# Attention projections laid out evenly, the next input converted a period earlier, and half of the value strips moved to the middle of a pair

## What is computed

```python
q = proj(wq, bq); k = proj(wk, bk); v = proj(wv, bv)          # x: 4 x 1024 x 512, 16 heads of 32
scores = jnp.einsum('bhqd,bhkd->bhqk', q, k) / scale
probs = jax.nn.softmax(scores, axis=-1)
ctx = jnp.einsum('bhqk,bhkd->bhqd', probs, v)
x = _layernorm(x + ctx.transpose(0, 2, 1, 3).reshape(B, S, HIDDEN) @ wo.T + bo)
x = _layernorm(x + ffn(x))      # top-2 of 8 experts, plus a gated shared expert
```

## Time and profile before

| what | value |
|---|---|
| median of three runs | 2179.62 us |
| the profiled execution | 2177.76 us |
| its span | 2176.0 us |
| PE busy | 2070.3 us, 95% |
| DVE, POOL, ACT busy | 1283.6, 880.2, 856.1 us |
| DMA | 205.91 MB |

### The profile page before, as it was taken

The page is one execution under the profiler, slowest core; times in us unless marked ns, Lnnn a source line. Parts: engine busy times, 40 slices in busy tenths (PEclk is TensorE's granted clock), DMA queues, the critical chain, the costliest instruction groups (busy, mean ns, idle before and its releaser), DMA issues. The chain is left out here.

```text
span 2176.0 us, 29929 instructions
## 1 busy us (share of the span) xinstructions
PE 2070.3 (95%) x9636; PEld 1208.4 (56%) x9637; DVE 1283.6 (59%) x2247; ACT 856.1 (39%) x1506; POOL 880.2 (40%) x852
## 2 busy tenths in 40 slices
PE   7999999999999999999999988789999999999997
PEld 5655555555555555455555433468744444446886
DVE  5777776577776477777477854456222222224875
ACT  2265554365554265554266663321111111112332
POOL 2254754454854454754354554400111111113651
PEclk9999999999999999999999999899999999999999
DMA  5321434212433312433303302661222222224752
GB/s 164 69 54 41 103 74 100 100 42 52 103 74 91 110 27 68 103 74 77 123 19 66 74 11 91 220 271 49 87 88 91 91 87 87 92 87 141 230 181 73
DMA packets 94816, 205.91 MB, mean 95 GB/s; under 512 B 24608, under 2 KB 25120, under 8 KB 92256
## 3 DMA queue, kind: packets, MB, share of 16 engines
q1 hardware_dynamic: 83888, 168.90, 26.6%
q0 software_dynamic: 10800, 35.40, 6.0%
HBM read 113.53 MB, written 39.85 MB: 70 GB/s over the span
## 5 line engine op out<-in xcount | busy, mean ns | idle before, releaser
L826 DVE TENSOR_REDUCE max_half<-ps_side 128x1 f32<-128x512 f32 x1024 | 668.7, 683 | 235.0 <-PE ps_side L584 231.8
L744 ACT ACTIVATE probs_outer<-ps_s 128x512 f32<-128x512 f32 x646 | 375.8, 599 | 245.5 <-PE ps_s L606 212.1
L606 PE MATMUL ps_s<-kq_stack 97*128 97x512 f32 x962 | 412.4, 431 | 15.2 <-ACT probs_mid L744 8.6
L584 PE MATMUL ps_side<-kq_stack 96*128 96x512 f32 x1024 | 404.0, 403 | 3.8 <-DVE max_half L826 2.4
L606 PEld LDWEIGHTS ps_s<-kq_stack 97*128 97x128 f32 x962 | 182.2, 189 | 206.7 <-issue 115.1
L1490 PE MATMUL ps_gu<-gu_sb,xT_e 128*128 x568 | 257.7, 596 | 0.5 <-issue 0.3
L1388 POOL DMA_INDIRECT x_g<-x,who_all x71 | 67.3, 948 | 454.6 <-PE ps_t L1480 358.4
L744 ACT ACTIVATE probs_mid<-ps_s 128x512 f32<-128x512 f32 x316 | 182.1, 599 | 128.9 <-PE ps_s L606 111.5
L522 POOL TENSOR_TENSOR acc<-probs_outer,probs_mid 128x512 f32<-128x512 f32 x129 | 163.5, 1296 | 154.7 <-ACT probs_mid L744 154.3
L584 PEld LDWEIGHTS ps_side<-kq_stack 96*128 96x128 f32 x1024 | 195.0, 190 | 49.7 <-DVE max_half L826 14.6
L522 POOL TENSOR_TENSOR acc<-probs_outer 128x512 f32<-128x512 f32 x129 | 162.8, 1289 | 138.8 <-ACT probs_outer L744 137.7
(11 more groups left out here) (210 smaller groups left out, 3037.0 us busy)
## 6 DMA issues: line engine op xcount, KB each, us to landing
kq_stack<-kq SPq DMA_DIRECT2D x192, 256.0 KB, 5.1
y_slots<-y_t SPq DMA_DIRECT2D x71, 256.0 KB, 2.3
res<-inv_rows SPq DMA_DIRECT2D x128, 64.0 KB, 2.0
probs_outer<-x SPq DMA_DIRECT2D x16, 512.0 KB, 5.1
x_r<-x SPq DMA_DIRECT2D x32, 256.0 KB, 3.6
x_t<-x SPq DMA_DIRECT2D x32, 256.0 KB, 3.2
gu_sb<-wgu SPq DMA_DIRECT2D x8, 1024.0 KB, 15.5
out<-gu_sb SPq DMA_DIRECT2D x32, 256.0 KB, 2.8
```

The costliest lines, as they stand in the source:

```text
L584: nc.tensor.matmul(bank, q_stack[par][0:3 * HD, h, t * P:(t + 1) * P], k_stack[par][0:3 * HD, h, half * HALF:(half + 1) * HALF], start=Tru ...
L606: nc.tensor.matmul(out, k_stack[par][0:3 * HD + 1, h, kt * P:(kt + 1) * P], q_stack[par][0:3 * HD + 1, h, half * HALF:(half + 1) * HALF], ...
L744: nc.scalar.activation(probs(loc, h), score_bank(b, loc * HG + h)[0], ACT.Exp, scale=HD ** -0.5).then_inc(probs_ready, 1)
L826: nc.vector.reduce_max(max_half[:, u // 2, u % 2:u % 2 + 1], bank, AX.X).then_inc(side_free, 1)
```

## The change

It does four things. The projection units are laid on the slots by a table `UNITS`, the same for all periods that project: three units over 16 slots each (not on every fourth slot), the fourth on slots 49 to 55. Each unit then ends on the last slot of a pair, and `low` stands right at the unit's end. `weighted` of a pair's first step (an even step) stands after slot 0 of the second step, the fifth of the pair's eight slots. Between a period's last projection product and the next period's first, the bank `ps_proj` is lent to the scores as a third bank. And the next x: the high copies move from POOL to ACT (`x_part`, at the places `X_HIGH`), the first four chunks are taken in steps 8 to 11 of period 1, before the weights, the other four in period 2; `normalise` of the first half moves from step 11 to step 15.

```diff
@@ -31,19 +31,22 @@
 PRE = NHALF * BLOCK_PRE
 SLOTS = 4
+FOLD = 2
+EARLIER_AFTER = 0
 UNIT = 3 * C
-SPREAD_OUT = (1, 14, (0, 1, 2, 3, 4, 4, 5, 6, 7, 8, 9, 10))
-DENSE = (9, 11, (0, 1, 1, 2, 3, 3, 4, 5, 5, 6, 7, 7))
-LOW_LATER = 2
+EVEN = (1, 2, 3, 5, 6, 7, 9, 10, 11, 13, 14, 15)
+UNITS = (*([first + slot for slot in EVEN] for first in (0, 16, 32)),
+         (49, 49, 50, 50, 51, 51, 52, 52, 53, 53, 54, 55))
+assert all(unit[-1] % (FOLD * SLOTS) == FOLD * SLOTS - 1 for unit in UNITS)
 ROW_SLOTS = (40, 63)
-PRE_TWICE = (15, 31, 47)
+PRE_TWICE = (12, 28, 44)
 PRE_UNTIL = 61
 INVERT = (36, 24)
-FOLD = 2
 PROBS = 3
 FOLD_DVE = 1
-NORM_AFTER, SPLIT_W_AFTER = (11, 9), 13
-X_AFTER = {(1, 15): (0, 1), (2, 1): (2, 3), (2, 3): (4, 5), (2, 5): (6, 7)}
+NORM_AFTER, SPLIT_W_AFTER = (15, 9), 13
+X_HIGH = {(1, 8): 0, (1, 9): 1, (1, 10): 2, (1, 11): 3, (2, 1): 4, (2, 2): 5, (2, 4): 6, (2, 5): 7}
+X_AFTER = {(1, 9): (0,), (1, 11): (1, 2, 3), (2, 1): (4,), (2, 3): (5,), (2, 5): (6, 7)}
 EXPS_BETWEEN = {3: ((0, 0), (0, 1)), 4: ((0, 2),), 5: ((0, 3), (1, 0), (1, 1)), 6: ((1, 2),), 7: ((1, 3),)}
...
-    if proj:
-        start, unit_slots, of_unit = proj
-        for i in range(PROJ * UNIT):
-            slot = start + unit_slots * (i // UNIT) + of_unit[i % UNIT]
-            plan[slot].append(("proj", i))
-            if i % UNIT == UNIT - 1:
-                plan[slot + LOW_LATER].append(("low", i // UNIT))
+    for u, unit in enumerate(proj):
+        for r, slot in enumerate(unit):
+            plan[slot].append(("proj", u * UNIT + r))
+        if unit:
+            plan[unit[-1]].append(("low", u))
...
-PLAN, PLACE, SIDE = side_plan(SPREAD_OUT)
-PLAN_NEW_X, PLACE_NEW_X, _ = side_plan(DENSE)
-PLAN_LAST, PLACE_LAST, _ = side_plan(None)
+PLAN, PLACE, SIDE = side_plan(UNITS)
+PLAN_LAST, PLACE_LAST, _ = side_plan(())
...
+LEND, RETURN = UNITS[-1][-1] + 2, STEPS * SLOTS + UNITS[0][0] - 4
...
 def score_banks(last):
+    banks, held, returned = [], {0: None, 1: None}, {}
+    proj = RING + SIDE_RING
     for i in range(G * STEPS * HG):
-        if last and i == HG * ((G - 2) * STEPS + 1):
-            held[RING + SIDE_RING] = None
-        if last and i == HG * ((G - 1) * STEPS + 1):
+        g, slot = divmod(i - HG, STEPS * SLOTS)
+        if slot == LEND and not (last and g >= G - 2):
+            held[proj] = None
+        if slot == RETURN and proj in held and not (last and g >= 1):
+            returned[g + 1] = held.pop(proj)
+        if last and (g, slot) == (G - 1, 0):
             held.update({RING + j: None for j in range(SIDE_RING)})
         bank = min(held, key=lambda k: -1 if held[k] is None else held[k])
         banks.append((bank, held[bank]))
         held[bank] = i
-    return banks
...
+(BANKS, RETURNED), (BANKS_LAST, RETURNED_LAST) = score_banks(False), score_banks(True)
...
-                    if g == 1:
-                        sp.wait_ge(x_split, b * CHUNKS + 2 * CHUNKS)
+                    if g == 0:
+                        sp.wait_ge(x_split, (b + 1) * CHUNKS + 3 + sel)
+                    elif g == 1:
+                        sp.wait_ge(x_split, (b + 1) * CHUNKS + CHUNKS - 1 + sel)
...
-                        sp.wait_ge(w_split, 2 * n + i + 1)
+                        sp.wait_ge(w_split, 2 * (n - 1) + i + 1)
+                    elif i in (4, 5):
+                        sp.wait_ge(w_split, 2 * n + i - 3)
...
@@ -357,27 +371,28 @@
                                  inv_rows[h].partition_broadcast(HD)).then_inc(rinv_in, 16)
             def body(b, m, g, last):
+                x_chunks = g == 1 and not last
+                if x_chunks:
+                    load_x(b + 1, m + 3, range(2))
                 if g:
                     invert((b * G + g) * NHALF - 1)
                 if g == 0:
                     sp.wait_ge(x2_out[7], 16 * (b + 1))
                     sp.sem_inc(passed_sp, 1)
                 invert((b * G + g) * NHALF, g == 0)
+                if x_chunks:
+                    load_x(b + 1, m + 3, range(2, 4))
                 if not (last and g == G - 1):
                     row(m, g, 0, last)
                 if not (last and g > 0):
                     load_w(b, m + 3, (g + 3) % G)
-                x_chunks = g == 1 and not last
-                if x_chunks:
-                    load_x(b + 1, m + 3, range(2))
                 if not last and g == G - 1:
                     sp.wait_ge(pv_done, (b + 1) * BSTEPS - FOLD)
                     sp.wait_ge(sum_done, (b + 1) * SUMS - 1)
                     sp.sem_inc(passed_sp, 1)
                     sp.dma_start(wv_lo[:].bitcast(F32), wv_lo_kept).then_inc(wv_moved, 16)
                 if not (last and g >= G - 2):
-                    spread(m + 2, g % 2, m, {h: lambda i=h + 1: load_x(b + 1, m + 3, [i])
-                                             for h in (1, 2)} if x_chunks else {})
+                    spread(m + 2, g % 2, m)
                 if not (last and g == G - 1):
                     row(m, g, 1, last)
                 if x_chunks:
...
@@ -466,13 +481,13 @@
                     split(wkq_hi[:, sel], wkq_lo[:, sel], stage[:, sel, :].rearrange("p (c o) -> p c o", c=C),
                           w_high, 2 * n + sel + 1, w_split)
-            def split_x(b, chunks):
+            def x_low(b, chunks):
+
                 for i in chunks:
-                    c, half = i % C, i // C
-                    pool.wait_ge(x_in[i % 2], 16 * ((b - 1) * (CHUNKS // 2) + i // 2 + 1))
-                    pool.sem_inc(passed, 1)
-                    at = (slice(None), c, slice(half * HALF, (half + 1) * HALF))
-                    split(x_hi[at], x_lo[at], stage[:, i % 2, :], x_high, b * CHUNKS + i + 1, x_split)
+                    at = (slice(None), i % C, slice(i // C * HALF, (i // C + 1) * HALF))
+                    pool.wait_ge(x_high, b * CHUNKS + i + 1)
+                    nc.gpsimd.tensor_tensor(x_lo[at], stage[:, i % 2, :], x_hi[at].bitcast(F32),
+                                            ALU.subtract).then_inc(x_split, 1)
             def projected(n):
...
+                    if r == 0 and i == 0 and g in returned_by(b):
+                        pe.wait_ge(probs_ready, b * HEADS_B + returned_by(b)[g] + 1)
...
-                    pe.wait_ge(proj_free, PROJ * B * G)
+                    pe.wait_ge(proj_free, PROJ * (b * G + (loc - 1) // STEPS + 3))
...
                         for kind, u, place in side_in(last, loc, slot):
                             side_unit(b, b * G + g, g, kind, u, place)
+                        if slot == EARLIER_AFTER and loc % FOLD == FOLD - 1:
+                            for done in range(loc - FOLD + 1, loc):
+                                weighted(b, done)
                         if slot == SLOTS - 1 and loc % FOLD == FOLD - 1:
-                            for done in range(loc - FOLD + 1, loc + 1):
-                                weighted(b, done)
+                            weighted(b, loc)
                             row_sums(b, loc)
             for i in range(2):
...
+            def x_part(b, i):
+                n = (b - 1) * G + 3
+                act.wait_ge(x_in[i % 2], 16 * ((b - 1) * (CHUNKS // 2) + i // 2 + 1))
+                act.wait_ge(proj_ready, PROJ * n + (PROJ // NHALF if i < C else PROJ))
+                nc.scalar.activation(x_hi[:, i % C, i // C * HALF:(i // C + 1) * HALF], stage[:, i % 2, :],
+                                     ACT.Copy).then_inc(x_high, 1)
...
+                    if (g, loc % STEPS) in X_HIGH and not last:
+                        x_part(b + 1, X_HIGH[g, loc % STEPS])
```

More of the change, by code:

```diff
@@ L99, in score_banks @@
         held[bank] = i
-    return banks
-BANKS, BANKS_LAST = score_banks(False), score_banks(True)
+    return banks, returned
+(BANKS, RETURNED), (BANKS_LAST, RETURNED_LAST) = score_banks(False), score_banks(True)
 def attention(nc, x, xT, wkqT, wvT, woT, bq, bk, bv, bo, x2, passed):
@@ L186, in score_bank, with returned_by @@
             return ps_s[:, bank, :] if bank < RING else ps_side[:, bank - RING, :], bank, before
+        def returned_by(b):
+            return {} if b < 0 else RETURNED_LAST if b == B - 1 else RETURNED
         const_in = sem("const_in")
@@ L274, in side_in @@
                 return []
-            return (PLAN if g != G - 2 else PLAN_LAST if last else PLAN_NEW_X)[i]
+            return (PLAN_LAST if last and g == G - 2 else PLAN)[i]
         def places(last, g):
-            return PLACE if g != G - 2 else PLACE_LAST if last else PLACE_NEW_X
+            return PLACE_LAST if last and g == G - 2 else PLACE
         def prologue():
@@ L316, in load_x, with spread @@
                                      "a p t -> (a p) t")).then_inc(x_in[i % 2], 16)
-            def spread(n, par, m=None, between={}):
+            def spread(n, par, m=None):
                 sp.wait_ge(proj_free, PROJ * (n + 1))
@@ L328, in spread @@
                                      kq[h * HD:(h + 1) * HD, parts, :].bitcast(F32)).then_inc(stacked[h], 16)
```

(4 more changed lines are left out.)

1 line of the change is left out of this document (removed).

## The result

The changed kernel takes 2187.13 us (median of 7 runs, 2185.15 to 2191.34). The kernel before, run beside it, takes 2179.62 (7 runs, 2177.28 to 2182.81). The ratio is 1.0035, with a 95% interval of 1.0023 to 1.0046: slower by a third of a per cent. In the medians the change is +7.5 us.

What follows compares the result with a forecast made beforehand. PE's matmuls and waits bound the kernel. Normal periods cancel; 3 x 3.9 + 3 x 0.3 - 0.5 - 2.4 = +9.7 us on the profiled 2177.76, with the median 1.9 higher, gives 2189; 8-in-10 range 2168 to 2199.

Steps and rivals of the forecast that it cites:

- the likeliest case: Whole kernel: slower, since ACT's wait for chunk 4 holds up PE; 2183 to 2196 us, chance 0.55.
- first rival: Start of period 2, batches 0 to 2: ACT's wait for chunk 4 is hidden, 21.6 us fall away, 2168; chance 0.18.
- Chunk 4, the term that decides: Period 2, batches 0 to 2: ACT's copy waits for a late load, exponentials queue behind it, PE stands still 5.4 us.
- Slow clock: Period 2, after PE's standstill: PE runs at its lower clock for a stretch, costing 1.8 us, bounds 0 to 3.4.
- Period 2 as a whole: Batches 0 to 2: 68.7 + 5.4 + 1.8 - 72.0 = +3.9 us each, a normal period plus standstill and slow clock.
- The price of a run of strips: Middle strips in each pair: every added run costs 0.33 us by its ends, 2.6 us per period.
- Nothing in the last period: Last period: added runs cost nothing, because PE waits anyhow at the pair's end.
- Stalls removed: Normal period: even layout and lent bank remove 2.4 + 0.7 = 3.1 us of PE's stalls.
- the lent bank: End of a period: the third bank helps the scores of slots 57 to 60, removing 0.7 us of stall.
- POOL's wait at the last sums: End of periods that split weights: POOL's fold is late and PE waits 0.4 to 0.5 us, bounds 0 to 1.4.
- Chunk 3 and the last batch's period 1: Period 1: ACT's wait for chunk 3 costs 0.3 us per batch; the last batch, without `split_w`, gains 0.5.
- Period 2 of the last batch: Two shorter runs spread DVE's maxima: +2.6 us for runs, 1 of 6 of stalls left, net -2.4 (-3 to 0).

Runs made afterwards that it cites:

- x_later: The changed kernel with ACT's high copies of chunks 4 to 7, and POOL's low parts with them, two steps later: 2168.51 us, ratio 0.9943.
- load_first: Experiment 2: the changed kernel with the loads of chunks 4 and 5 issued ahead of the copies to `kq_stack`: 2171.48 us, ratio 0.996.
- no_mid: Experiment 3: the changed kernel without middle runs, both steps' value strips together at a pair's end: 2164.16 us, ratio 0.9927.
- mid_alone: The kernel before with the middle runs of strips added and nothing else: 2203.37 us, ratio 1.011.
- x_low_moved: As 9, with chunk 3's low part behind step 13's fold and chunk 5's right behind chunk 4's: 2136.36 us, ratio 0.9808 against the kernel before.
- experiment 7: `x_later` without middle runs, the third score bank lent only from the last batch's period 1 on: 2151.07 us, ratio 0.9879.
- 6: `x_later` with the last pair's fold of each period shared, two heads on POOL and two on DVE: 2177.15 us, ratio 0.9993.
- 9: `x_later` with middle runs only in the last batch's period 2 and high copies moved to where PE is at strips: 2148.02 us, ratio 0.9865.

## Why the prediction was right, point by point

The forecast was 2189, the measurement 2187.1, and the likeliest case was the one that came. The mechanism that decides, the wait for chunk 4, is shown; that the total fits so closely is luck, as the points below say. Its first rival (the wait for chunk 4 is hidden, 2168) is what `x_later` made true, at 2168.5, though by 18.6 us off 2187.1 and not by 21.6 off 2189.

- **Chunk 4, the term that decides: right in mechanism and in each of its times.** The load was put at 10.9 into the period and came at 10.88; the landing at 13.6 and came at 13.7; slot 10's score at 14.9 and came at 14.90 (577.12 - 562.22). The standstill was put at 5.4: it is 5.35 from start to start, 5.1 over the normal distance. Slow clock was put at 1.8: from 577.12 to the strips at 580.98 nine matmuls take 3.86 us; at 0.234 each and 0.09 before the strips they would take 2.2, so 1.7 over. The pair takes 15.42 where 8.63 is normal, +6.8 of the 7.2 expected; in the two other batches +8.0 and +7.8. `x_later` and `load_first` show the cause from both ends. One reading in it was incomplete: that the copies to `kq_stack` are limited by issue and landing at 1.2 us each, whatever else runs. From 562.22 to 571.80, with most of them under way, the DMA engines are 0.97 busy. So the bytes of the copies (256 KB each) fill the engines, and the load's place behind twelve of them is a place behind 3 MB:

```profile
562.22:571.80 9.58, 9.58 (x55) 5.37 (x51) 6.14 (x10) 5.17 (x9) 3.94 (x4) 1.00 0.97 208
```

- **Period 2 as a whole: +3.9 forecast, +4.85, +3.5 and +5.0 measured.** The gain set against the standstill was right: without it the period would take 75.47 - 6.8 = 68.7, as forecast. What is over comes from the two batches with longer waits.
- **The price of a run of strips: right in size, and its transfer from the earlier trace rows to a run of 8 strips is shown.** 0.29 to 0.36 per pair in `no_mid`, 0.30 to 0.34 in six of the eight pairs of `mid_alone` and less in two, 2.25 per period in both against 2.6. For the whole kernel the size holds less well, as experiment 3 has it: 23 us instead of 37. "Nothing in the last period" is right too (43.46 without the runs, 43.37 with them).
- **Stalls removed: mis-sized, by an error that cancelled another.** 3.1 was put on them; the normal period of `x_low_moved`, 66.10, says 2.58. Within it the lent bank is worth 0.23 by the trace of experiment 7, not 0.7: three banks keep slots 57 to 60 going, but the last score still waits 0.45 for an exponential. That leaves 2.35 for the layout, where 2.4 was counted.
- **POOL's wait at the last sums: right in size (0.39 against 0.4 to 0.5), wrong as an addend.** Pair 7 with middle run and POOL's wait is 7.50, without both 7.14, a difference of 0.36 where 0.33 + 0.39 would be 0.72. The middle run gives some of it back in the same place: without it the transposition comes 0.59 after the last score (537.35 to 537.94), waiting for DVE's last maximum, and with it 0.34 (559.43 to 559.77), when DVE was done before the score. So normal periods were -3.1 + 2.6 + 0.5 on paper. In the traces they are -2.6 for the stalls, +2.2 for the runs of pairs 0 to 6 and +0.4 for pair 7, its run and POOL's wait together. The sum was right and its parts were not.
- **Periods 0 and 3: not told apart from period 1 in the sum.** They gained 0.4 to 1.0 each, the last period 1.2; together 4.8 us where nothing was forecast. Against them stand +1.7 in period 2, +1.5 in the last batch's period 2 (below), 1.3 in the prologue and 0.9 outside the periods, none of it forecast; the total fits to 0.4 us because these offset each other, and that is luck.
- **Chunk 3 and the last batch's period 1: near.** 0.3 per batch was put on chunk 3, and periods 1 changed by +0.8, +0.1 and +0.2; the last batch's gave -0.85 for -0.5.
- **Period 2 of the last batch: mis-sized, -0.9 for -2.4.** I had left 1 us of 6 for stalls. The middle runs do help there, 0.94 by experiment 3, so the direction is shown; but by the prediction's own count (53.6 of work and 2.6 for the added runs) 2.5 us of stalls stay in the 58.69, where 1 was left.
- **The prologue: +1.3 us that no step foresaw.** It is 1.1 to 2.8 us longer than before in every trace of a kernel with the change; the cause stays open.

## What to carry to other kernels

When a wait is moved into an engine's in-order list, date both ends: when the engine gets there, and when the thing lands, which is set by all that stands ahead of its issue in the queue. Here the six or seven microseconds between the two cost more than everything that the move was to bring, and shifting the waiting instruction by two steps gave it back. Price what is split by the number of runs, not by the work in it; and when one wait is removed, read the same stretch again on the other engines, since in three of these experiments (2, 6, 9) the wait came back on a neighbour.
